# One stage for the last message-passing layer, the normalization after it and the node projections of a graph network

## What is computed

```python
for _ in range(3):
    msgs = relu(h[src] @ W_edge + b_edge)
    agg = segment_sum(msgs, dst)
    h = relu(concat([agg, h]) @ W_agg + b_agg)
x = layernorm(x + h)
q, k, v = x @ Wq + bq, x @ Wk + bk, x @ Wv + bv
...
h1 = ln(agg1 + x @ Wskip + bskip + x)
```

## Time and profile before

| what | value |
|---|---|
| median of 3 runs | 6480.81 us (6471.52 to 6483.21) |
| profiled execution | 6482.03 us, span 6480.2 us |
| busy over the span | PE 71%, PEld 44%, DVE 58%, ACT 29%, POOL 54% |
| granted TensorE clock, mean | 0.784 of 2.4 GHz |
| DMA | 840.28 MB moved, mean 130 GB/s |

### The profile page before, as it was taken

One profiled execution on the slowest core, in us unless ns is written; L12 is line 12 of the kernel. 1 busy time (PEld: TensorE's weight loads), 2 busy tenths in 40 slices (PEclk: granted clock), 3 DMA queues, 4 the chain that ended last, 5 costly groups with the idle time before them and its releaser, 6 DMA issues. The chain is left out here.

```text
span 6480.2 us, 105856 instructions
## 1 busy us (share of the span) xinstructions
PE 4587.8 (71%) x19910; PEld 2854.0 (44%) x19911; DVE 3774.3 (58%) x12450; ACT 1885.8 (29%) x4118; POOL 3525.7 (54%) x3741
## 2 busy tenths in 40 slices
PE   5666657777777777666666777466666666888887
PEld 3444445555555555444443333244444443333333
DVE  7666633333333333333347888577777776777777
ACT  0222223333333333011110000122222222666665
POOL 1555554444344443544434555666666653888887
PEclk9888878888878888777788999655555555999999
DMA  1333345545455454333336888433333332333333
GB/s 34 127 126 124 131 126 149 155 149 153 148 149 151 149 154 146 112 109 108 108 102 220 266 270 268 149 89 88 91 91 88 88 85 69 101 104 104 104 106 96
DMA packets 732213, 840.28 MB, mean 130 GB/s; under 512 B 150205, under 2 KB 575272, under 8 KB 732068
## 3 DMA queue, kind: packets, MB, share of 16 engines
q1 hardware_dynamic: 619172, 619.89, 29.9%
q0 software_dynamic: 112896, 218.94, 13.4%
HBM read 439.86 MB, written 398.61 MB: 129 GB/s over the span
## 5 line engine op out<-in xcount | busy, mean ns | idle before, releaser
L762 POOL DMA_INDIRECT mp_gathered<-msg_rows,other_idx x1176 | 1120.9, 953 | 1411.5 <-PE bank L781 902.1
L781 PE MATMUL bank<-mp_edge_hot,mp_gathered 128*128 128x256 bf16 x5292 | 933.6, 308 | 458.6 <-issue 400.7
L781 PEld LDWEIGHTS bank<-mp_edge_hot,mp_gathered 128*128 x5292 | 560.9, 106 | 743.6 <-issue 637.9
L840 ACT ACTIVATE mp_h_out<-bank,mp_b_agg 128x256 f32<-128x256 f32 x588 | 278.7, 474 | 1429.6 <-PE bank L799 749.3
L525 POOL DMA_INDIRECT by_window<-so_pay,so_pos_i x392 | 395.2, 1008 | 437.6 <-issue 305.5
L1206 POOL DMA_INDIRECT at_kv<-kv_rows,kv_idx x392 | 422.1, 1077 | 348.1 <-DVE at_v_e L1355 241.5
L874 DVE TENSOR_SCALAR mp_edge_hot<-digits,mp_first_col,column 128x256 bf16<-128x256 bf16 x1764 | 506.1, 349 | 109.6 <-issue 74.8
L799 PE MATMUL bank<-mp_h_in,mp_w_agg_h 128*128 128x256 f32 x1176 | 474.0, 491 | 109.1 <-issue 103.7
L897 DVE TENSOR_TENSOR mp_msg_out<-mp_rest,mp_msg_out 128x256 bf16<-128x256 f32 x392 | 166.3, 424 | 650.2 <-ACT mp_msg_out L853 393.2
L1490 POOL DMA_INDIRECT ff_agg<-at_rows,last_idx x392 | 414.1, 1056 | 96.7 <-issue 89.0
L1208 POOL DMA_INDIRECT at_q<-q_rows,node_idx x392 | 393.5, 1004 | 126.7 <-issue 126.7
(11 more groups left out here) (217 smaller groups left out, 9283.4 us busy)
## 6 DMA issues: line engine op xcount, KB each, us to landing
mp_h_in<-h_cols SPq DMA_DIRECT2D x588, 128.0 KB
h_cols<-mp_h_out SPq DMA_DIRECT2D x588, 128.0 KB
msg_rows<-mp_msg_out SPq DMA_DIRECT2D x392, 192.0 KB
kv_rows<-pn_proj SPq DMA_DIRECT2D x98, 512.0 KB
msg_rows<-so_msg_out SPq DMA_DIRECT2D x98, 384.0 KB
h_cols<-so_h_out SPq DMA_DIRECT2D x98, 256.0 KB
pn_h_in<-h_cols SPq DMA_DIRECT2D x98, 256.0 KB
x_rows<-pn_x_b SPq DMA_DIRECT2D x98, 256.0 KB
```

Source lines behind the costliest of these rows:

```text
L762: pool.indirect_dma_start(gathered[:, r * PARTS * D:(r + 1) * PARTS * D], None, core.msg_rows[layer % 2], bass.IndirectOffsetOnAxis(ap=cor ...
L781: product = nc.tensor.matmul(agg_bank[k], gathered[:, bass.ds(at + d * D, D)], hot, start=(first and d == 0), stop=True, skip_group_check= ...
```

## The change

`message_passing` now runs two layers. A new stage `last_layer` does the third layer, the edge counts, the normalization and the projections together; `project_nodes` is gone, and `last_edges` comes after the new stage. `h_cols` is not written in the last layer and not read back.

- In the sum over edges the operands change places: the 0/1 matrix is stationary, in two halves of 128 destinations, and the gathered tile is the moving one with 128 columns. The result has nodes on partitions. A tile takes six products.
- The bias of the aggregation is laid into the bank by a product with ones at the start of a group of two blocks. VectorE does relu and adds x in one instruction (`add_rows`).
- The root is taken by ScalarE (`roots`), and five small VectorE instructions make the reciprocal deviation and a shift (`deviations`). ScalarE normalizes (`normalize`) and evicts two of the four projection tiles, whose bias TensorE has laid in (`evict`, `BY_ACT`); VectorE evicts the other two. The identity is added to Wskip, so that x itself comes out of the product.
- GpSimd only gathers. Rings are deeper (8 for the 0/1 matrices, 4 for h, for the counting matrices and for groups), and lags go up to ten blocks.

```diff
 message_passing:
-                for layer in range(LAYERS):
+                for layer in range(LAYERS - 1):
...
 last_layer, TensorE:
+            def add_tile(r, i, hot):
+                at = (i & (TILES - 1)) * (PARTS * D)
+                for half in range(2):
+                    to = rows_bank[r // 2 % 2][:, (r % 2 * 2 + half) * P:(r % 2 * 2 + half + 1) * P]
+                    for d in range(PARTS):
+                        product = nc.tensor.matmul(to, hot(half), gathered[:, bass.ds(at + d * D, D)], start=False, stop=True, skip_group_check=True)
+                return product
...
+                if r % 2 == 0:
+                    reached(pe, y_ok, Q * j + r // 2 - 1)
+                    nc.tensor.matmul(rows_bank[r // 2 % 2][:, :], core.ones[0:PARTS, :], agg_parts[:, :], start=True, stop=True, skip_group_check=True)
+                pe.wait_ge(edge_hot_ok, n + 1)
+                pe.wait_ge(tile_in, first + ALWAYS)
+                for c in range(ALWAYS):
+                    added = add_tile(r, first + c, lambda half: edge_hot[r % HOTS][:, c, half * P:(half + 1) * P])
+                added.then_inc(tile_mm, 1)
+                further(pe, n, first, final, more)
+                pe.wait_ge(h_ld[r % RING], 16 * (TURN // RING * j + r // RING + 1))
+                for half in range(2):
+                    own = nc.tensor.matmul(rows_bank[...], h_in[r % RING][:, half * P:(half + 1) * P], w_agg_h[:, :], start=False, stop=True, skip_group_check=True)
+                own.then_inc(block_mm, 1)
...
+            def project(g, q, j):
+                pe.wait_ge(cols_ok, g + 1)
+                for t in range(T):
+                    if t < T - BY_ACT:
+                        reached(pe, by_dve, (T - BY_ACT) * (g - 1) + t + 1)
+                    else:
+                        reached(pe, by_act, BY_ACT * (g - 1) + t - (T - BY_ACT) + 1)
+                        nc.tensor.matmul(proj_bank[t][:, :], core.ones[0:PARTS, :], proj_parts[:, :], start=True, stop=True, skip_group_check=True)
+                    nc.tensor.matmul(proj_bank[t][:, :], x1_cols[q % 2][:, t * P:(t + 1) * P], weights[:, :], start=t < T - BY_ACT, stop=True, ...)
+            def turn(do):
+                do(0, sum_edges)
+                do(0, count_targets)
+                do(-6, group(turn_x1))
+                do(-8, group(project))
 last_layer, ScalarE:
+            def turn(do):
+                do(0, group(roots))
+                do(-4, group(x1_columns))
+                do(-2, group(normalize))
+                do(-6, group(evict))
 last_layer, VectorE:
+            def add_rows(g, q, j):
...
+                nc.vector.scalar_tensor_tensor(out=y[q][:, :, :], in0=rows_bank[q % 2][...], scalar=0.0, in1=x_in[q][:, :, :], op0=ALU.max, op1=ALU.add).then_inc(y_ok, 1)
+                dve.wait_ge(y_ok, g + 1)
+                norm_stats(nc, dve, stat_c, g, y[q], stats[q], moments[q]).then_inc(mom_ok, 1)
+            def turn(do):
+                do(-3, group(add_rows))
+                do(-6, group(deviations))
+                do(-8, group(add_b2))
+                do(-10, group(add_biases))
+                do(0, hots)
+                do(0, target_hots)
 build:
+        last_layer(core, a["L0_gnn_W_agg"], a["L0_gnn_b_agg"], a["x"], l1, l1)
+        core.end_stage()
         last_edges(core)
-        core.end_stage()
-        project_nodes(core, a["x"], l1, l1)
```

More of the change, by code:

```diff
@@ L772, in _ @@
                 pe.wait_ge(wts, 5 * 16)
[L773 to L776, removed]
+                for layer in range(LAYERS - 1):
+                    wins, turns_done = layer * NW, layer * (NW // RING)
                     def add_tile(k, i, hot, first=False):
@@ L812, in messages @@
                         product.then_inc(m_mm, 1)
[L814 to L820, removed]
                     def turn(do):
                         do(0, sum_edges)
[L824 to L828, removed]
+                        do(-1, edge_product)
+                        do(-2, messages)
                     blocks(pe, turn, MSGS)
@@ new lines, in last_layer, with rows, blocks, straight @@
+        x1_t, cols_ok, mm, by_dve, by_act = (core.sem("ll_" + n) for n in (
+            "x1_transposed", "x1_cols_ready", "product", "proj_by_vector", "proj_by_scalar"))
+        def rows(t, g):
+            return t[g * GR:(g + 1) * GR, :].rearrange("(p k) f -> p k f", k=T)
+        def blocks(eng, turn):
+            def straight(n):
+                def do(lag, step):
+                    if 0 <= n + lag < NW:
+                        step(n + lag, (n + lag) % TURN, (n + lag) // TURN)
+                turn(do)
+            for n in range(2 * TURN):
+                straight(n)
+            with aligned(eng, 2, NW // TURN) as j:
+                for r in range(TURN):
+                    turn(lambda lag, step: step(TURN * j + r + lag, (r + lag) % TURN, j + (r + lag) // TURN))
+            for n in range(NW // TURN * TURN, NW + 2 * TURN):
+                straight(n)
@@ new lines, in group, with at_second_block, edge_tiles @@
+        def group(step):
+            def at_second_block(n, r, j):
+                if r % 2:
+                    step(Q * j + r // 2, r // 2, j)
+            return at_second_block
+        words = {}
+        def edge_tiles(eng, n, r):
+            if r == 0:
+                words[eng.engine] = nc.values_load_multi_w_load_instructions(
+                    core.spans[0:1, bass.ds(n, TURN)], engines=[eng.engine], min_val=0, max_val=512 * NT - 1,
+                    skip_runtime_bounds_check_because="both halves are masked and only address tables of their size")[1]
+            word = words[eng.engine][r]
+            return word & 511, word >> 9
@@ L963, in project_nodes, with further @@
+        def further(eng, n, first, last, more):
+            with eng.If(first + (ALWAYS - 1) < last):
+                before = eng.value_load(core.more_before[0:1, bass.ds(n, 1)], min_val=0, max_val=NT - 1)
+                with eng.Fori(first + (ALWAYS - 1), last) as i:
+                    more(i, (before + i - (first + (ALWAYS - 1))) & 511)
         block = s.enter_context(nc.Block())
-        def rows(t, g):
-            return t[bass.ds(g * GR, GR), :].rearrange("(p k) f -> p k f", k=T)
@@ L1004, in _ @@
         @block.tensor
         def _(pe):
[L1006 to L1019 removed]
+            pe.wait_ge(wts, 14 * 16)
```

356 lines of the change are left out of this document (215 added, 141 removed).

## The result

The changed kernel takes 6169.8 us (median of 4 runs, 6163.8 to 6181.5) where the kernel before takes 6482.0 beside it (4 runs, 6471.5 to 6491.1): ratio 0.9521, 95% interval 0.9501 to 0.9541. It is faster by 312 us; 164 were forecast, with a range that holds the result.

What follows compares the result with a forecast made beforehand. TensorE's sequencer, slowed by gathers, was taken to set the pace: 2 x 8.6 + 7.2 + 2.9 = 27.3 us a chunk, 49 chunks 1338 us, plus 27 = 1365 us; 6482 - 1528 + 1365 = 6319, so 6318 us; range 6110 to 6475 us.

Steps and rivals of the forecast that it cites:

- six products a tile instead of three add nine steps a block: New stage, TensorE's sequencer: nine more register steps at 0.125 us raise a block from 2.44 to 3.6 us.
- 3 to 4 us less a chunk: New stage, bound on TensorE's sequencer: what a chunk saves if the second half reuses the gathered tile's address.
- the burst with its clock: New stage, each chunk: 7.2 us for the gathers' effect on TensorE's sequencer plus 2.9 us for the lowered clock.
- The pace: New stage, undisturbed: TensorE's sequencer takes 8.6 us a group of two blocks, 2 x 8.6 us a chunk.
- The burst: New stage: ten microseconds of gathers slow TensorE's sequencer and cost 7.2 us a chunk, as read from the old last layer.
- 27 us around the loop: New stage's start (loads of weights and biases, first gathers) and the drain of the ten-block lag: 27 us together.
- The array by lines: New stage, TensorE's array: edge products, transposes, projection and bias products sum to 8.2 to 8.7 us a group.
- the text's own signs: Profile signs: bursts about 27 us apart, twice the register steps per block; wrong if under 23, over 31, or TensorE awaits matrices.
- Static products fill the gathers: Rival, chance 0.20: each gather burst hides one projection and the clock stays up; 22.8 us a chunk, kernel 6098 us.
- The projections come once in two blocks, wherever the burst happens to be: New stage: objection to the rival in which static products fill the gathers, that projections are not tied to the bursts.
- The slow steps vanish: Rival, chance 0.07: 688 ns register steps belong to the old loop alone; 18 us a chunk, stage 909, kernel 5863 us.
- The gathers disturb longer: slower: Rival, chance 0.13: added stores share the DMA engines and lengthen bursts; at 17 us of gathers 32.4 us a chunk, 6569 us.

Runs made afterwards that it cites:

- experiment 3: Changed kernel with the gathered tile's address worked out anew for the second half: 6405.6 us, ratio to the kernel before 0.988, stage 1406 us.
- experiment 5: Changed kernel without the four products a block that count the nodes' edges in the new stage: stage 1140 us (total 5974.3 us, not comparable).
- Experiment 1: Changed kernel with the new stage's gathers left out after the first ring of 32 tiles: 5912.8 us, stage 924 us.
- experiment 2: Kernel before the change, with the third layer's gathers left out after the first ring of 32 tiles: 6210.9 us, that layer's edge products 555 us.
- experiments 1 and 6: Experiment 1, and the changed kernel with a plain copy in place of each indirect gather in the new stage: 5734.0 us, stage 908 us.
- the other chip: Changed kernel there with chunks of four: 5440.4 us; with reports one chunk later too: 4909.0; that with chunks and reports of two: 4996.3. Stages 925, 910, 908 us.

## Why the prediction was right or wrong

Right: the sign, that TensorE would bound the stage and no other engine, that the gathers' effect on its sequencer is a large term, and the sizes of what is hidden.

In part the forecast was lucky. Its mechanism of pace is wrong, and so is its largest loss; that 6318 came no further from 6170 owes something to errors of opposite sign.

**The step that failed in the mechanism** is "six products a tile instead of three add nine steps a block". The trace shows nine a block, not eighteen; experiment 3, which adds them and six index steps, takes 233 us more in the stage. So the array paces an undisturbed group, not the sequencer. The text had the case as a bound, "3 to 4 us less a chunk", that is 23.3 to 24.3 us, and measured are 23.9. But this bound does not follow from the text's own terms. With the address reused the sequencer would come to 2 x 2.44 + 1.4 = 6.3 us a group, and then the array, put at 8.2 to 8.7 us, binds: 0.8 us less a chunk at most, and not 3 to 4. Nor is 6.3 right: that the sequencer takes half of what is saved in experiment 5, with a shortest group of 8.75 us, says that its own work per group is near that.

**The term that carries the miss** is the burst with its clock, 7.2 + 2.9 = 10.1 us a chunk. Experiment 1 measures 5.1 for both together. Step by step:

- The pace: 2 x 8.6 us forecast, 2 x 9.21 measured, 1.2 us more a chunk.
- The burst: 7.2 us forecast. That figure came from an undisturbed block of 2.44 us, where 2.83 is the mean (experiment 2), and the old layer really loses 5.5 a chunk, its low clock included. To add 2.9 for the clock was to count part of it twice. By the table of losses the new stage loses 3.9 while steps are slow and 1.8 while the clock is low.
- So 27.3 + 1.2 = 28.5 would have been the chunk with the burst as forecast; with 5.1 to 5.5 in place of 10.1 it is 23.5 to 23.9, and 23.9 was measured.
- 27 us around the loop were 52.
- The array by lines, from start to start in undisturbed groups: 36 edge products 2.02 (0.056 each; half of 0.109 was taken), own terms 1.00 and counts 0.87 (1.74 taken), transposes 0.44 (as taken), the projection 3.93 (3.4 taken: the short one), bias products 0.95 (0.65 taken). Together 9.21.

Of the text's own signs, bursts 24.1 us apart lie in its 23 to 31, and TensorE's waits for VectorE's matrices are 13 us in all; twice as many register steps per block did not appear.

On the 128-column product the trace contradicts the Trainium skill (TensorE: Matmul & The Clock Gate, Back-to-back issue gap): 0.056 us a pair of load and product, sustained over 18 of them, where the page has about 81 ns for sustained pairs (0.056 us is what it gives for a product by itself). The measurement decides.

VectorE was forecast at 8.3 us a group and has 777.79 / 98 = 7.9; ScalarE at 3.7 and has 355.58 / 98 = 3.6; the DMA share at 0.52 and is 0.59. All hidden, as the waits show.

**The rivals.** *Static products fill the gathers* came closer than the forecast: 22.8 us a chunk and 6098 us, where 23.9 and 6170 were measured and the forecast had 27.3 and 6318. Its picture is in the trace: 37 of 47 bursts begin with a group's transposes, so that the projection fills the first five microseconds. "The projections come once in two blocks, wherever the burst happens to be" was the objection, and it does not hold, since GpSimd's wait ties most bursts to the end of a group's edge products. But the clock does not stay up, and the slow steps come behind the projection. How much of the gain is this alignment's and how much comes from the burst itself stays open. *The slow steps vanish* put the stage at 18 us a chunk, 909 us. This is what experiments 1 and 6 and the other chip show: 908 to 925 us. The change itself was not run on that chip, so its gain there stays open. *The gathers disturb longer: slower* did not happen: the DMA share was 0.59 against the 0.38 of the old layer, and the gathers cost 5.1 us a chunk against 5.5.

## What to carry to other kernels

Before pricing an address worked out at run time by the number of instructions that use it, count how many distinct addresses a block has: the same expression in a second loop over halves cost nothing here, and worked out anew it cost 233 us. When an engine idles for nothing that the profile names, sort its losses by the time since the burst that goes with them; here the first six microseconds of indirect gathers were free in the new stage and the next six were not, and bursts of half the length took most of the loss away. Look also at what the burst is tied to: most began with products whose addresses are fixed. And run on more than one chip: where no step was slow, the change and the halving together brought next to nothing (0.996). And an issuing loop that waits for its newest transfer before the next gives up its own queue: waiting for the one before it brought the ratio from 0.996 to 0.899 on one chip, and gave 0.883 against 0.904 where steps are slow (on two different chips).

## What the runs showed of the hardware that was not expected

- TensorE's register steps for the edge products, 46 ns as a rule, reach 0.7 us and more from six microseconds into a burst of eight indirect gathers by GpSimd in the new stage, and from three in the old layers. In bursts of four gathers they hardly do (3 of 2424 over 100 ns), and not in bursts of eight plain copies of the same bytes (51 ns at most), which are over in 4.3 us.
- This depends on the chip or its state: beside the runs in which the kernel before takes 6290 to 6480 us they are there; where it takes 5463, no register step of the edge products is over 65 ns. The sort stage (817 against 628 us) and attention (1325 against 1113 us) of the same kernel with chunks of four differ too. One chip also changed between two batches, 6482 to 6292 us for the kernel before, with the slow steps there in both. The cause was not found.
- With less array work the clock was lower, not higher: 0.88 instead of 0.91 without the counting products, in a stage that still pauses once per burst. Slow steps were more in that run too (120 instead of 71), so the pauses were longer; which brought which is not shown.
